# Retention stage: the q row scale moved into the clip bounds, q taken out of PSUM by ACT, the sine product done by Pool

## The reference, cut to what matters

```python
q = xf @ Wq.T ; k = xf @ Wk.T * SCALING ; vr = xf @ Wv.T        # heads of 32
qr = q * cos + rotate_every_two(q) * sin                        # kr likewise
mask = exp(d * decay); mask = mask / sqrt(mask.sum(-1, keepdims=True))
qk = einsum('bhqd,bhkd->bhqk', qr, kr) * mask
den = clip(abs(qk).sum(-1, keepdims=True), 1.0, 50000.0)
out = einsum('bhqk,bhkd->bhqd', qk / den, vr)
out = (out - out.mean(-1)) / sqrt(out.var(-1) + 1e-5) * ln_g + ln_b
x = x + gelu(out) @ Wo.T
```

## Time and profile before

| what | us |
|---|---|
| median of 3 runs | 2621.92 (2620.39 to 2627.72) |
| the profiled execution | 2624.51 |
| its span, first to last instruction | 2622.4 |
| retention stage, first scores to last instruction | about 41 to 1123 |

### The profile page before, as it was taken

One profiled execution on the slowest core, in us unless ns is written; L12 is line 12 of the kernel. 1 busy time (PEld: TensorE's weight loads), 2 busy tenths in 40 slices (PEclk: granted clock), 3 DMA queues, 4 the chain that ended last, 5 costly groups with the idle time before them and its releaser, 6 DMA issues. The chain is left out here.

```text
span 2622.4 us, 43895 instructions
## 1 busy us (share of the span) xinstructions
PE 2512.7 (96%) x15328; PEld 1786.7 (68%) x15328; DVE 1834.2 (70%) x2847; ACT 1449.9 (55%) x2044; POOL 517.6 (20%) x444
## 2 busy tenths in 40 slices
PE   5999999999999999979999969999999999999999
PEld 2444444444444444369999958888888888888888
DVE  4878777777777777657777757666666666666665
ACT  2666565566566566636566545555555555555554
POOL 2333333333333333201212110000000000000000
PEclk8999999999999999989999979999999999999999
DMA  6232222222232222123223143000000000000000
GB/s 233 51 85 60 77 62 79 65 72 75 56 85 59 83 59 70 49 71 111 82 77 115 49 146 106 18 24 24 18 23 24 24 24 24 24 24 24 24 17 16
DMA packets 116786, 157.95 MB, mean 60 GB/s; under 512 B 16272, under 2 KB 82328, under 8 KB 116384
## 3 DMA queue, kind: packets, MB, share of 16 engines
q1 hardware_dynamic: 116640, 156.01, 20.1%
HBM read 72.03 MB, written 33.59 MB: 40 GB/s over the span
## 5 line engine op out<-in xcount | busy, mean ns | idle before, releaser
L488 DVE TENSOR_TENSOR l_prod<-l_scores,l_window 128x1024 f32<-128x1024 f32 x512 | 615.6, 1218 | 220.7 <-PE l_scores L325 186.0
L679 ACT ACTIVATE l_absp<-l_prod 128x1024 f32<-128x1024 f32 x512 | 521.9, 1053 | 282.8 <-PE l_den L350 233.6
L1696 ACT ACTIVATE e_r<-e_h,e_bn,e_rs 128x512 f32<-128x512 f32 x512 | 399.4, 781 | 485.7 <-PE e_h L1547 484.5
L325 PE MATMUL l_scores<-l_qst,l_kst 96*128 96x512 f32 x1024 | 369.3, 457 | 27.9 <-DMA l_qst<-l_lo 12.0
L325 PEld LDWEIGHTS l_scores<-l_qst,l_kst 96*128 96x128 f32 x1024 | 167.4, 190 | 288.3 <-issue 147.9
L1547 PE MATMUL e_y<-e_whi,e_h2lo 128*128 128x256 f32 x1024 | 289.8, 283 | 0.0
L1546 PE MATMUL e_y<-e_wlo,e_h2hi 128*128 128x256 f32 x1024 | 289.7, 283 | 0.0
L1545 PE MATMUL e_y<-e_whi,e_h2hi 128*128 128x256 f32 x1024 | 289.2, 282 | 0.1
L350 PE MATMUL l_den<-l_absp,l_ones 128*32 128x512 f32 x2048 | 274.7, 609 | 0.0
L339 PE MATMUL l_num<-l_prod,l_v 128*32 128x512 f32 x2048 | 269.3, 598 | 0.0
L1791 DVE CAST e_h1hi<-e_r 128x512 fp32r<-128x512 f32 x256 | 111.2, 434 | 224.3 <-ACT e_r L1696 220.2
(11 more groups left out here) (191 smaller groups left out, 4472.2 us busy)
## 6 DMA issues: line engine op xcount, KB each, us to landing
l_kst<-l_hi SPq DMA_DIRECT2D x256, 64.0 KB, 2.0
l_qst<-l_hi SPq DMA_DIRECT2D x256, 64.0 KB, 2.0
l_raw<-in_xT SPq DMA_DIRECT2D x8, 1024.0 KB, 5.6
l_kst<-l_lo SPq DMA_DIRECT2D x128, 64.0 KB, 2.0
l_qst<-l_lo SPq DMA_DIRECT2D x128, 64.0 KB, 2.0
l_xo<-in_x SPq DMA_DIRECT2D x32, 256.0 KB, 2.8
x_scratch<-l_xo SPq DMA_DIRECT2D x32, 256.0 KB, 2.3
l_xr<-x_scratch SPq DMA_DIRECT2D x8, 1024.0 KB, 8.0
```

Of the source, the lines that this page charges most:

```text
L325: mm = nc.tensor.matmul(sc[j][:, s, :], kst[g][0:96, h, 128 * kt:128 * kt + 128], qst[c][0:96, h, :], start=True, stop=True)
L488: nc.vector.tensor_tensor(prod[n % 4][:], sc[j][:], win[:, 4 * g + 2 * j:4 * g + 2 * j + 2, w0:w0 + QC], ALU.mult).then_inc(prod_ready, 1)
L679: nc.scalar.activation(absp[n % 4][:], prod[n % 4][:], ACT.Abs).then_inc(abs_ready, 1)
L1696: nc.scalar.activation(r[m][:], p[m][:], ACT.Relu, bias=bn_[layer][1][:, m, e:e + 1], scale=rs[layer][:, m, e:e + 1]).then_inc(done, 1)
```

## The change

Five edits, all in the retention stage. The table `rowscale` goes, and a table `clip` of 128 x 128 numbers comes: lower and upper bounds for each phase. DVE's reading of the denominators becomes two dependent instructions, a max and a min, and PE's wait for bank A is for the first of them (`den_floor`). ACT takes q out of bank A with scale 1.0, with the function that took k. DVE's multiplication by the sine goes, and POOL does it, ahead of the cosine. The head of the stage, which prepares the first k and q before the steps begin, is changed in the same way.

```diff
@@ -240,7 +240,7 @@
                     pe.wait_ge(geps_ready, b + 2)
                 else:
-                    pe.wait_ge(den_ready, 4 * b if before == "dT3'" else 4 * b + int(before[2]) + 1)
+                    pe.wait_ge(den_floor, 4 * b if before == "dT3'" else 4 * b + int(before[2]) + 1)
 
@@ -456,25 +456,11 @@
         def _(dve):
 
-            def q_rotate_in(n, a, g, c):
-
-                if not isinstance(n, int) or n > 0:
-                    dve.wait_ge(lo_ready, n)
-                dve.wait_ge(a_ready, a + 1)
-                nc.vector.tensor_tensor(t1[:].rearrange("p (a b) -> p a b", b=32), pA[:].rearrange("p (a b) -> p a b", b=32),
-                                        rsc[:, g, CROWS * c:CROWS * c + CROWS].unsqueeze(2).to_broadcast([128, CROWS, 32]),
-                                        ALU.mult).then_inc(t1_ready, 1)
-
             def shuffle(n):
 
                 dve.wait_ge(t1_ready, n + 1)
                 dve.sem_inc(waited, 1)
                 nc.vector.stream_shuffle(t2[:], t1[:], [i ^ 1 for i in range(32)]).then_inc(shuffled, 1)
-
-            def rotate_sin(n, c):
-
-                dve.wait_ge(shuffled, n + 1)
-                nc.vector.tensor_tensor(t2[:], t2[:], sin_sb[:, QC * c:QC * c + QC], ALU.mult).then_inc(rot_ready, 1)
@@ -504,10 +490,12 @@
             nT_A = pA[:].rearrange("p (m d) -> p m d", d=32)
 
-            def take_den(a):
+            def take_den(a, phase, p):
 
                 dve.wait_ge(a_ready, a + 1)
-                nc.vector.tensor_scalar(dent[:], nT_A[:, :, 0], 1.0, 50000.0, ALU.max, ALU.min).then_inc(den_ready, 1)
+                nc.vector.tensor_tensor(dent[:], nT_A[:, :, 0], bounds[:, 0, p, :], ALU.max).then_inc(den_floor, 1)
+                dve.wait_ge(den_floor, phase + 1)
+                nc.vector.tensor_tensor(dent[:], dent[:], bounds[:, 1, p, :], ALU.min).then_inc(den_ready, 1)
 
@@ -565,10 +553,7 @@
             dve.wait_ge(tables_in, 16 * NTABLES)
             for n in range(3):
-                if n == 1:
-                    q_rotate_in(1, 4, 0, 0)
                 shuffle(n)
-                rotate_sin(n, n // 2)
             dve.wait_ge(consts, 16 * NCONST)
 
@@ -589,11 +574,11 @@
                     if kt == 2 and prep_q:
                         shuffle(nq)
-                    if kt == 3 and post:
-                        take_den(A("dT" + tag))
-                        head_sums(Bn("nT" + tag))
                     if kt == (7 if p == 2 else 6) and prep_k:
                         shuffle(nk)
+                    if kt == 3 and post:
+                        take_den(A("dT" + tag), ph, 3 if prev else p - 1)
+                        head_sums(Bn("nT" + tag))
                     if not last:
@@ -608,16 +593,10 @@
                         add_residual(Bn("o1'"), 1, 4 * b - 2, 16 * (2 * b - 1))
-                    if kt == 1 and prep_q:
-                        q_rotate_in(nq, A(f"q{p}"), g, c)
-                    if kt == 2 and prep_q:
-                        rotate_sin(nq, (p + 1) % 2)
                     if kt == 3 and post:
                         centre(ph)
                     if kt == 4 and post:
                         variance(ph)
-                    if kt == (7 if p == 2 else 6) and prep_k:
-                        rotate_sin(nk, p % 2)
                     if not last:
@@ -651,12 +630,12 @@
         def _(act):
 
-            def k_take(n, a):
+            def take(n, a, scale):
 
                 if not isinstance(n, int) or n > 0:
                     act.wait_ge(lo_ready, n)
                 act.wait_ge(a_ready, a + 1)
-                nc.scalar.activation(t1[:], pA[:], ACT.Copy, scale=SCALING).then_inc(t1_ready, 1)
+                nc.scalar.activation(t1[:], pA[:], ACT.Copy, scale=scale).then_inc(t1_ready, 1)
 
             def high(n, before, count):
@@ -704,12 +683,13 @@
 
-            k_take(0, 2)
+            take(0, 2, SCALING)
             v_take(3, 0, 0, 1)
             high(0, None, 0)
+            take(1, 4, 1.0)
             v_take(5, 0, 1, 2)
             high(1, k_stacked[0], STACK)
-            k_take(2, 6)
+            take(2, 6, SCALING)
             high(2, q_stacked, STACK)
@@ -729,11 +709,13 @@
                     if kt == 3 and post:
                         squares(A("dT" + tag), ph)
+                    if kt == 1 and (p < 3 or not last):
+                        take(prep_order(f"q{p}", b), A(f"q{p}"), 1.0)
                     if kt == 3 and (p < 3 or not last):
                         high(prep_order(f"q{p}", b), *before(f"q{p}", b))
                     if (p < 2 or not last):
                         if kt == (6 if p == 2 else 5):
-                            k_take(prep_order(f"k{p}", b), A(f"k{p}"))
+                            take(prep_order(f"k{p}", b), A(f"k{p}"), SCALING)
                         if kt == 7:
@@ -760,9 +742,10 @@
             pool.wait_ge(made, NMADE)
 
-            def rotate_cos(n, c):
+            def rotate(n, c):
 
                 pool.wait_ge(shuffled, n + 1)
+                nc.gpsimd.tensor_tensor(t2[:], t2[:], sin_sb[:, QC * c:QC * c + QC], ALU.mult).then_inc(rot_ready, 1)
                 nc.gpsimd.tensor_tensor(t1[:], t1[:], cos_sb[:, QC * c:QC * c + QC], ALU.mult).then_inc(cos_ready, 1)
@@ -1890,14 +1873,16 @@
     window = gamma[None, :, None, None] ** dist * factor[None, :, None, :]
-    rowscale = np.stack([factor[4 * g + np.arange(128) // 32] for g in range(2)], 1)
+    tok, t, head = np.arange(128)[:, None, None], np.arange(4)[None, :, None], np.arange(4)[None, None, :]
+    scale = np.stack([factor[4 * (p // 2) + head, (512 * (p % 2) + 128 * t + tok) // R].reshape(128, 16) for p in range(4)], 1)
+    clip = np.stack([1.0 / scale, 50000.0 / scale], 1)
     angle = np.repeat(1.0 / 10000.0 ** np.linspace(0.0, 1.0, 16), 2)
     turn = (i[:, None] + i[None, :]).reshape(-1)[None, :] * angle[:, None]
     sine = np.sin(turn)
     sine[0::2] *= -1
     tri = np.arange(128)
```

More of the change, by code:

```diff
@@ L18, with layer0 @@
 F32R = mybir.dt.float32r
-def layer0(nc, x, xT, wqT, wkT, wvT, woT, lng, lnb, window, rowscale, cosT, sinT, avg8, ident, x1):
+def layer0(nc, x, xT, wqT, wkT, wvT, woT, lng, lnb, window, clip, cosT, sinT, avg8, ident, x1):
     B, L, E = x.shape
@@ L76, in layer0 @@
         win = sb("window", [128, H, (2 * ROWS - 4) * 32])
-        rsc = sb("rowscale", [128, 2, ROWS])
+        bounds = sb("clip", [128, 2, PHASES, 16])
         cos_sb, sin_sb = sb("cos", [128, L]), sb("sin", [128, L])
@@ L122, in layer0 @@
         n_taken, d_taken, nsum_ready, centred = sems("n_taken d_taken nsum_ready centred")
-        sq_ready, den_ready, var_ready, fac_step = sems("sq_ready den_ready var_ready fac_step")
+        sq_ready, den_floor, den_ready, var_ready, fac_step = sems("sq_ready den_floor den_ready var_ready fac_step")
         on_ready, z_ready, o_added = sems("on_ready z_ready o_added")
@@ L144, in _ @@
                 sp.dma_start(dst, src).then_inc(weights_in, 16)
-            for dst, src in ((sin_sb[:], sinT), (cos_sb[:], cosT), (rsc[:], rowscale)):
+            for dst, src in ((sin_sb[:], sinT), (cos_sb[:], cosT), (bounds[:], clip)):
                 sp.dma_start(dst, src).then_inc(tables_in, 16)
@@ L644, in _ @@
             centre(4 * B - 1)
-            take_den(a_order("dT3'", B - 1, False, "after"))
+            take_den(a_order("dT3'", B - 1, False, "after"), 4 * B - 1, 3)
             variance(4 * B - 1)
@@ L808, in _ @@
             pool.wait_ge(tables_in, 16 * NTABLES)
-            rotate_cos(0, 0)
+            rotate(0, 0)
             split(0)
             low(0, None, 0)
-            rotate_cos(1, 0)
+            rotate(1, 0)
             split(1)
             low(1, k_stacked[0], STACK)
-            rotate_cos(2, 1)
+            rotate(2, 1)
             split(2)
@@ L824, in body @@
                     if p < 3 or not last:
-                        rotate_cos(prep_order(f"q{p}", b), (p + 1) % 2)
+                        rotate(prep_order(f"q{p}", b), (p + 1) % 2)
                         split(prep_order(f"q{p}", b))
@@ L832, in body @@
                     if p < 2 or not last:
-                        rotate_cos(prep_order(f"k{p}", b), p % 2)
+                        rotate(prep_order(f"k{p}", b), p % 2)
                         split(prep_order(f"k{p}", b))
@@ L1876, in program @@
     layer0(nc, I["x"], I["xT"], I["wqT0"], I["wkT0"], I["wvT0"], I["woT0"], I["ln_g"], I["ln_b"], I["window"],
-           I["rowscale"], I["cosT"], I["sinT"], I["avg8"], I["ident"], x1)
+           I["clip"], I["cosT"], I["sinT"], I["avg8"], I["ident"], x1)
     with nc.sbuf_tensor("feat", [128, L // 128, E], F32) as feat:
@@ L1899, in shape_constants @@
     out = {
-        "window": window.reshape(128, H, -1), "rowscale": rowscale, "cosT": np.tile(np.cos(turn), (4, 1)),
+        "window": window.reshape(128, H, -1), "clip": clip, "cosT": np.tile(np.cos(turn), (4, 1)),
```

## The result

The changed kernel takes 2641.32 us (median of 4 runs, 2640.05 to 2643.45) against 2623.28 us before in the same session: a ratio of 1.0068, with a 95% interval of 1.0055 to 1.0081. It is 18.0 us slower. The profiled execution has a span of 2639.9 us, 17.5 us more than before.

What follows compares the result with a forecast made beforehand. PE's own work was taken to set the pace in nearly every step. The terms 19.6 + 0.9 + 0.4 + 0.9 + 2.4 = 24.2 us, on 2621.9, gave 2646 us, range 2635 to 2662.

Steps and rivals of the forecast that it cites:

- Part 1: ACT's q take queues behind kt = 1's absolute values, delaying PE's transposes: 23 x 0.85 = 19.6 us, plus phase 3's 0.9.
- Part 2: DVE loses its q moves and sines, 79 us of busy time, but PE sets the pace: nothing counted as gain.
- Part 3: Max and min replace one clip on the denominators: 0.4 us, only in phases 2 and 3 of the last batch element.
- the block: Rival: DVE's min, both operands in SBUF, waits out a POOL instruction; 2682 us, or 2664 with half; chance 0.07.
- Part 4: POOL's sine makes its sum at most 1.5 us later, still in time; only the head costs, 0.9 us.
- Part 5: New idle time before phase 2's group-sum wait brings one or two more falls of TensorE's clock: 2.4 us.

Runs made afterwards that it cites:

- e4: Changed kernel with ACT taking q twice in a row, the second take waiting for the first; 2673.34 us, ratio to before 1.0186.
- e3: Changed kernel with the sine product back on DVE, ACT's late take and max and min kept; 2639.60 us, ratio to before 1.0062.
- e10: Changed kernel with only the min moved behind the centring of kt = 3; 2640.67 us, ratio to before 1.0067.
- e1: Changed kernel with ACT's take of q moved ahead of both absolute values of kt = 1; 2631.14 us, ratio to before 1.0031.
- e6: e1 with the sine back on DVE and the min left right behind the max; 2621.91 us, ratio to before 1.0004.
- e2: Changed kernel with DVE instead of ACT taking q, at DVE's old place; 2638.58 us, ratio to before 1.0053.
- e5: e1 with the min moved behind the centring of kt = 3; 2620.84 us, ratio to before 0.9997.
- e9: e2 with the min moved behind the centring of kt = 3; 2623.63 us, ratio to before 1.0003.
- e11: Changed kernel with early take, max ending kt = 2, min behind centring, phase 3's k rounding ahead of take_num, head sine on DVE; 2605.97 us, ratio to before 0.9935.

## Why the prediction was right

*Part 1, the take behind the absolute values*, was right to the hundredth: 4.16 us from `den` to the transposes against 3.33, and 4.75 us for the step instead of 3.86. Over the 23 phases that is 20.4 us against 19.6. Phase 3: 7 x 0.15 = 1.1 us against 0.9. e4 shows that the take's length goes into the step in full, e3 and e10 that neither the sine nor the min is the cost, and e1 shows it gone.

*Part 2, nothing for DVE's relief*: right. PE's plain steps stayed at 2.98 us. DVE's busy time fell by 59 us, not by the 75 I named; I had added up printed durations (their sum fell by 73), which overlap a little. In e6 the sine is back and costs nothing.

*Part 3, max and min*: right in sum for the changed kernel, since the min took 0.18 us as a median. PE's second score half of kt = 4 waited visibly for DVE only in the two phases of the last batch element that I had priced (0.51 and 0.35 us of idle time, where it had been 0.15 and 0.14); their steps are 0.6 us longer together, against 0.4. But on the block I was lucky. I placed the min 0.1 us ahead of the end of POOL's sum; it came 0.14 us ahead of it (498.71 against 497.56 + 1.29) and was not held up, because the block was over by then, which I did not know. Some tenths earlier it would have been, as in e1, where this took back half of the gain. And I wrote that the old trace neither shows nor excludes the block, when the sine's 0.90 us beside POOL and 0.69 without it were in it.

*Part 4, POOL's sine*: right within the steps (its sum held up nobody). In the head the first scores come 0.8 us later (42.14 against 41.38), I said 0.9; counted from ACT's first take it is 24.8 us in the kernels with the sine on POOL in the head and with ACT's take of q, and 24.0 before and in e3 and e6, where DVE does it.

*Part 5, the clock*, was the wrong term: I added 2.4 us for one or two more falls. In the stage the profile after has 2 falls behind the head where before had 4, and the steps with the group sums are 2.1 us shorter together. An idle time of 0.67 us ahead of the transposes brought none. The other kernels with the late take and nothing added, e3 and e10, had 1 and 2 falls, those with the transposes of phases 0 to 2 on time (e1, e2, e5 to e9, e11) 1 to 5: no more with the idle time than without.

*The sum.* My terms without the clock came to 21.8 us; in the profiled executions they are 20.4 + 1.1 + 0.6 + 0.8 = 22.9. The 18.0 us of the medians (14.4 to 21.2 by the interval) are less. Between the two profiled executions the rest is 1.9 us more for the DMA, 2.1 less in the steps with the group sums, 1.7 less at the loop boundaries and 2.2 less behind the stage. Nothing differs behind the stage in any of these kernels, and the 13 profiled executions took from 1513.5 to 1519.4 us there, the one before 1519.1. So this part is how one execution differs from the next, and that the total came out below my forecast and not above it is not to the forecast's credit. The loop boundaries I did not test: they took 44.8, 43.9 and 44.0 us in all in the changed kernel, e3 and e10, 46.5 before and 44.7 to 49.5 in the kernels with the transposes on time, so a part of the 1.7 us may belong to the change.

## What to carry to other kernels

When a step is moved to an idle engine, look at what stands ahead of it in that engine's queue and what that waits for, not at how busy the engine is: ACT had 1.38 us free at this place, but behind the take's deadline. When a repair gives back less than it should, compare step by step which one grew, and look for short instructions that have become long, since a block between DVE and POOL is printed as duration. And where PE waits for what stands behind them, keep DVE instructions with two operands in SBUF away from POOL's work, even those of a few elements.

## What the runs showed of the hardware that I had not expected

A DVE operation on 128 x 16 numbers, both operands in SBUF, took 0.71 us when it started 0.61 us into a POOL instruction of 1.29 us, up to 1.19 us in e2, and 0.18 when it started 1.15 us into it; one on 128 x 2 took 0.70 where it takes 0.16. With one operand in PSUM it took 0.17 to 0.18 at the same place.

For TensorE's clock the length of an idle time did not decide by itself. In e4 1.82 us in phase 3 was followed by a stretch at 1.2 GHz six times of seven, 1.30 us never in 23. In the changed kernel 0.67 us (23 times) and 1.19 us (7 times, phase 3) were never followed by one, the wait of the group sums of up to 1.17 us (7 times) once, and the idle time of 1.7 to 2.2 us at the loop boundary (5 times) once. In the kernel before, the wait of the group sums, as long as now, was followed by one three times, and 2.3 us at the loop boundary was, 2.6 and 2.7 us were not.
